# Down products of a sparse expert layer turned round: 256 tokens wide, rounded 32-bit parts, gates applied ahead of the product

## The chip, the cores and the metric

The kernel runs on one core of one Trainium2 chip. A core has a matrix engine (TensorE, PE in the profile, with its weight loads as PEld), a vector engine (VectorE, DVE), an activation engine (ScalarE, ACT), a general engine (GpSimd, POOL) and a queue engine that issues DMAs (SyncE, SP). SBUF is the on-chip memory of 128 partitions, PSUM the eight accumulation banks that TensorE writes. The metric is the device time of one execution in microseconds; the kernel before takes 240.61 us, the median of 3 runs (240.35 to 241.06).

## The reference

One decoder layer on 8 sequences of 128 tokens of width 128, everything in 32-bit floats: causal self-attention with 16 heads, layer norm after the residual, cross-attention with 16 heads of 8, layer norm, then a layer of 8 experts of which a router picks two for each token, and a last layer norm. The part that matters here:

```
x2      = layernorm(x1 + cross_attention(x1, ctx))           # [1024 tokens, 128]
dense_w = sparsemixer(x2 @ router_w.T)                       # [1024, 8], two entries of a row are not 0
for e in range(8):
    h_e  = silu(x2 @ w_gate[e].T) * (x2 @ w_up[e].T)         # [1024, 256]
    out += dense_w[:, e:e+1] * (h_e @ w_down[e].T)           # [1024, 128]
result  = layernorm(x2 + out)
```

The kernel computes every expert for every token.

## The kernel before, in words

Each engine has one long list of calls, written out by hand and tied together by semaphores; nothing reorders them when the kernel runs. The calls are small helpers, and `n` or `l` in them is the sequence.

**Attention part.** Queries, keys and values are projected in three passes of rounded 32-bit numbers: a number is split into a rounded high part and the remainder, and high x high, high x low and low x high are added up in PSUM. Plain 32-bit products do scores, mixing and transposes. The eight sequences are interleaved, self-attention of one beside cross-attention of another. In `normalise_x1` (line 835) VectorE turns `res1` in SBUF into `x1` in SBUF.

**Expert part.** Tokens are taken in four chunks of 256 (`c`, of `NCH`). For each chunk there are 16 blocks of 128 hidden units, two to an expert (`FB`), so `gate_up(i)` runs 64 times (i from 0 to 63). It makes six products of 256 columns, three for the gate and three for the up half, into one bank. The first 32 (`NFILL`) stand in the list among the last calls of the attention part. ScalarE takes the silu of the gate half (`gate`, line 561), VectorE multiplies it with the up half from PSUM (`hidden`, line 935) into `hid`. For the first chunks `hid` lies where the raw weights and the query/key tiles were.

`down_product(c, e)` (line 1988) multiplies the hidden values of one chunk and one expert with the expert's down weights. The hidden values are the stationary side, 128 tokens at a time, and the moving side is 128 output columns wide, in plain 32-bit: four products for an expert, with tokens on the partitions of the result. `combine` (line 1320) on VectorE then multiplies a 128x128 result in PSUM with the gate, a number for each partition, and adds it to a sum in SBUF. In the last chunk the same is done in 16 pieces (`last_product`, line 2001, `combine_last`, line 1332). When a chunk's sum is complete, VectorE makes its statistics, GpSimd raises the variance to the power -1/2 (line 479), VectorE normalises and SyncE sends it out.

The router's choice is worked out once for all tokens by `rank_0` to `rank_9` on VectorE: some 30 steps on 128x64 values in SBUF, laid between the calls `hidden(17)` and `hidden(26)`. GpSimd has nothing to do in this part but `split_x2`, which splits the transposed x2 (lines 353 and 355), and the roots.

In the main loop TensorE makes one down product and two gate/up products in turn; VectorE combines in the same rhythm.

Of the kernel before, what the change touches and what calls it, by code (L numbers as in the profile page):

```python
# [5 lines left out]
F32 = mybir.dt.float32  # L6
F32R = mybir.dt.float32r
# [31 lines left out]
def build_decoder(nc, x, xT, ctxT, mask, wqT, wkT, wvT, woT, cwqT, cwkT, cwvT, cwoT, cbq, cbk, cbv, cbo,  # L39
# [12 lines left out]
    LAST, LAST_E = NCH - 1, 3  # L52
# [18 lines left out]
    NFILL = 32  # L71
    NTANH = 10

    with ExitStack() as ctx:
# [6 lines left out]
        def flat(t):  # L81
# [81 lines left out]
        dense_w = sb("dense_w", [P, B, E])  # L163
        NS = 4
        silu = sb("silu", [P, NS, CH])
        hid = [raw[:].rearrange("p (k t) -> p k t", k=KB),
               qk_a[:].rearrange("p b a k t -> p (b a k) t")]
        free_s = flat(probsT_s)
        acc = free_s[:, 0:2 * TB * D].rearrange("p (c a d) -> p c a d", c=2, a=TB)
        y_out = free_s[:, 2 * TB * D:3 * TB * D].rearrange("p (a d) -> p a d", a=TB)  # L170
# [7 lines left out]
        Y_BANK = [X0, T1, OC]  # L178
        MAIN_BANK = [Y1, X1, OS, T0]

        LAST_UNITS = [(tb, e) for e in range(LAST_E) for tb in range(TB)] + [(tb, e) for tb in range(TB) for e in range(LAST_E, E)]
        LAST_BANK = [Y_BANK[(LAST * E + u) % 3] for u in range(3)] + MAIN_BANK

        FILL_BANK = [Y0, Y1, OS, X1, OC, Y1, T0, X1, T1, Y0, OC, X1, T0, OC, X1, Y0,
                     T0, OS, Y0, X1, OS, X0, OC, T0, Y1, Y0, X1, T1, OS, T0, OC, Y0]
# [8 lines left out]
        def hid_of(b):  # L196
# [18 lines left out]
        (wo_s, res1_done, stat1_done, aggr1_done, var1_done, pow1_done, x1_ready, x1bo_done,  # L215
         x1T_ps, x1T_evac, cq_proj, cq_evac, cq_lower) = [sem(n) for n in (
             "wo_s res1_done stat1_done aggr1_done var1_done pow1_done x1_ready x1bo_done "
             "x1T_ps x1T_evac cq_proj cq_evac cq_lower").split()]
        (oc_evac, oct_ps, rec_c, ccat_done, ccatT_ps, ccatT_evac, wo_c, res2_done, stat2_done, aggr2_done, var2_done, pow2_done,
         x2_ready, x2T_ps, x2T_evac, logit_ps, logit_evac, x2_split) = [sem(n) for n in (  # L220
             "oc_evac oct_ps rec_c ccat_done ccatT_ps ccatT_evac wo_c res2_done stat2_done aggr2_done var2_done pow2_done "
             "x2_ready x2T_ps x2T_evac logit_ps logit_evac x2_split").split()]
        (r_step, r_exp_in, r_exp, dense_ready, gated, silued, gate_done, hid_done, down_ps, combined,
         stat3_done, aggr3_done, var3_done, pow3_done, y_ready) = [sem(n) for n in (
             "r_step r_exp_in r_exp dense_ready gated silued gate_done hid_done down_ps combined "
             "stat3_done aggr3_done var3_done pow3_done y_ready").split()]

        def qk_of(a, pair, which, i):

# [253 lines left out]
        def _(act):  # L483
# [276 lines left out]
            for i in range(2 * KB, NCH * KB):  # L760
                gate(i)
# [1304 lines left out]
```

## Time and profile before

| what | value |
|---|---|
| median of 3 runs | 240.61 us (240.35 to 241.06) |
| profiled execution | 241.12 us, span of the instructions 239.3 us |
| granted TensorE clock, mean | 0.997 |
| TensorE busy | 229.1 us (96%) |
| VectorE busy | 194.4 us (81%) |
| ScalarE busy | 165.7 us (69%) |
| GpSimd busy | 100.9 us (42%) |

TensorE's busy time counts the modelled length of each product, which overlaps the next one; how fast products really follow each other is read from the difference of their start times.
### The profile page before, as it was taken

What the parts mean: (1) busy time and instruction counts of PE and PEld (TensorE: products, weight loads), DVE (VectorE), ACT (ScalarE), POOL (GpSimd) and SP (SyncE); (2) the same over time, 40 slices, a digit from 0 to 9 for tenths busy, and PEclk for the clock granted to TensorE, in tenths of its full rate; (3) what the DMA queues carried; (4) which work ended last, traced back from release to release, by engine and by line L of the source; (5) the groups of instructions that cost most, each with busy time, mean ns of one, the idle gap of its engine ahead of it and who ended that gap; (6) DMA issues with size and microseconds to landing.
All of it is one profiled execution on the core that took longest, in us unless ns stands there. A gap on an engine that the chain in (4) does not pass through costs nothing.

```text
span 239.3 us, 6960 instructions
## 1 busy us (share of the span) xinstructions
PE 229.1 (96%) x2274; PEld 205.8 (86%) x2274; DVE 194.4 (81%) x955; ACT 165.7 (69%) x546; POOL 100.9 (42%) x159
## 2 busy tenths in 40 slices
PE   6899999999999999999999899999999999999992
PEld 6889888887888979978869668797999999999992
DVE  1897799988788889998898985998989755766885
ACT  2769678898989898989989989489448333333000
POOL 3386966465533569808384863302400000100111
PEclk9999999999999999999999999999999999999998
DMA  5997000000000000000000004000000000000000
GB/s 181 358 360 285 9 0 1 4 0 4 3 1 3 0 5 0 3 4 0 4 0 4 0 3 178 0 3 3 1 3 0 0 4 0 4 22 0 22 25 23
DMA packets 6723, 9.10 MB, mean 38 GB/s; under 512 B 1056, under 2 KB 5280, under 8 KB 6304
## 3 DMA queue, kind: packets, MB, share of 16 engines
q1 hardware_dynamic: 4176, 7.09, 8.3%
q10 hardware_dynamic: 2512, 1.57, 2.2%
q8 instruction: 18, 0.29, 0.5%
q14 instruction: 17, 0.14, 0.2%
HBM read 8.14 MB, written 0.52 MB: 36 GB/s over the span
## 4 chain that ended last, share of the span: by engine, by line
PE 83%; DVE 6%; issue 4%; POOL 2%; DMA 2%; ACT 1%; POOLq 0%; SPq 0%; DVEq 0%; ACTq 0%
PE bank L1501 11%; PE bank L1410 10%; PE bank L1411 9%; PE bank L1412 9%; PE bank L1988 7%; PE bank L1483 7%; PE bank L1510 6%; PE bank L1551 6%; PE bank L1494 3%; PE bank L1519 3%; DMA raw<-in_wqT 2%; PE bank L1526 2%; PE bank L1438 2%; PE bank L1440 1%; PE bank L1439 1%
## 5 line engine op out<-in xcount | busy, mean ns | idle before, releaser
L500 ACT ACTIVATE probs_s<-masked_s,nmax_s 128x128 f32<-128x128 f32 x128 | 50.1, 395 | 2.1 <-PE bank L1501 1.1
L296 POOL TENSOR_TENSOR probs_s<-probs_s,rec_sum_s 128x512 f32<-128x512 f32 x32 | 33.2, 1040 | 38.8 <-DVE rec_sum_s L812 38.8
L503 ACT ACTIVATE probs_c<-masked_c,nmax_c 128x128 f32<-128x128 f32 x128 | 40.8, 397 | 1.2 <-DVE nmax_c L805 1.0
L561 ACT ACTIVATE silu<-bank 128x256 f32<-128x256 f32 x54 | 20.3, 387 | 30.0 <-PE bank L1412 28.3
L1410 PE MATMUL bank<-ctx_hi,gu_hi 128*128 128x256 f32 x128 | 38.5, 300 | 0.0
L1411 PE MATMUL bank<-ctx_lo,gu_hi 128*128 128x256 f32 x128 | 35.8, 279 | 0.0
L1412 PE MATMUL bank<-ctx_hi,gu_lo 128*128 128x256 f32 x128 | 35.7, 279 | 0.0
L805 DVE CUSTOM_DVE_ANT_0 masked_c<-bank,mask_add 128x128 f32<-128x128 f32 x128 | 29.3, 286 | 3.7 <-PE bank L1494 2.2
L805 DVE CUSTOM_DVE_ANT_0 masked_s<-bank,causal 128x128 f32<-128x128 f32 x128 | 29.2, 286 | 2.2 <-PE bank L1483 1.8
L479 POOL TENSOR_TENSOR mv<-mv,minus_half 128x1 f32<-128x1 f32 x8 | 4.3, 548 | 58.6 <-DVE mv L1352 58.6
L1410 PEld LDWEIGHTS bank<-ctx_hi,gu_hi 128*128 128x128 f32 x128 | 24.2, 189 | 0.5 <-issue 0.4
L500 ACT ACTIVATION_READ_ACCUMULATOR probs_s<-masked_s,nmax_s 128x1 f32 x128 | 24.5, 191 | 0.0
L1411 PEld LDWEIGHTS bank<-ctx_lo,gu_hi 128*128 128x128 f32 x128 | 24.2, 189 | 0.0
L1412 PEld LDWEIGHTS bank<-ctx_hi,gu_lo 128*128 128x128 f32 x128 | 24.1, 188 | 0.0
L542 ACT COPY xT_all<-bank 128x512 f32<-128x512 f32 x32 | 18.3, 581 | 6.0 <-PE bank L1501 5.5
L1410 PE MATMUL bank<-x_hi,w_hi 128*128 128x256 f32 x64 | 19.9, 312 | 0.7 <-DVE w_lo L772 0.7
L1501 PE MATMUL bank<-ident,probs_c 128*128 128x128 f32 x128 | 19.5, 278 | 0.0
L1501 PE MATMUL bank<-ident,probs_s 128*128 128x128 f32 x128 | 19.0, 276 | 0.2 <-POOL probs_s L296 0.2
L1411 PE MATMUL bank<-x_lo,w_hi 128*128 128x256 f32 x64 | 18.0, 282 | 0.0
L1412 PE MATMUL bank<-x_hi,w_lo 128*128 128x256 f32 x64 | 18.0, 282 | 0.0
L935 DVE TENSOR_TENSOR qk_a<-silu,bank 128x256 f32<-128x256 f32 x32 | 12.8, 419 | 6.4 <-ACT silu L561 6.1
L1510 PE MATMUL bank<-probsT_s,v_sb 128*64 128x128 f32 x256 | 17.5, 279 | 0.0
(165 smaller groups left out, 589.3 us busy)
## 6 DMA issues: line engine op xcount, KB each, us to landing
raw<-in_gateT SPq DMA_DIRECT2D x1, 1024.0 KB, 8.6
raw<-in_upT SPq DMA_DIRECT2D x1, 1024.0 KB, 11.7
down_sb<-in_down SPq DMA_DIRECT2D x1, 1024.0 KB, 4.8
raw<-in_wvT SPq DMA_DIRECT2D x1, 512.0 KB, 6.3
ctxT_all<-in_ctxT SPq DMA_DIRECT2D x1, 512.0 KB, 7.6
wo_sb<-in_woT SPq DMA_DIRECT2D x1, 512.0 KB, 6.2
masked_c<-in_mask ACTq DMA_DIRECT2D x1, 512.0 KB, 11.2
x_tok<-in_x ACTq DMA_DIRECT2D x1, 512.0 KB, 9.8
```

The lines of the kernel that those rows point to most:

```text
L296: pool.tensor_tensor(probs_s[:, g % 2], probs_s[:, g % 2], spread(rec_sum_s[:, 4 * g:4 * g + 4], 2, S), ALU.mult).then_inc(normed[g], 1)
L500: last = act.activation(probs_s[:, g % 2, i, :], masked_s[:, g % 2, i, :], ACT.Exp, scale=-1.0, bias=nmax_s[:, h:h + 1], accum_out=rsum_s[ ...
L503: last = act.activation(probs_c[:, g % 2, i, :], masked_c[:, g % 2, i, :], ACT.Exp, scale=-1.0, bias=nmax_c[:, h:h + 1])
L542: act.copy(dst[:, g % 2].rearrange("p h t -> p (h t)"), b[:]).then_inc(turned_evac[kind][g], 1)
L561: act.activation(silu[:, i % NS, :], g, ACT.Silu).then_inc(silued, 1)
L805: last = dve.tensor_tensor_reduce(out=masked[:, g % 2, i, :], in0=b[:, i * S:(i + 1) * S], in1=add, scale=-1.0, scalar=3e38, op0=ALU.add, ...
L1410: pe.matmul(dst, wh, xh, start=True, stop=False)
L1411: pe.matmul(dst, wh, xl, start=False, stop=False)
L1412: return pe.matmul(dst, wl, xh, start=False, stop=True)
L1483: ins = pe.matmul((even, odd)[r][:, i * S:(i + 1) * S], qk_of(a, pair, 0, i)[rows, toks], qk_of(a, pair, 1, i)[rows, toks], start=True, st ...
L1501: last = pe.transpose(b[:, i * S:(i + 1) * S], (probs_s if kind == "s" else probs_c)[:, g % 2, i, :], ident[:])
L1510: last = pe.matmul(b[DQ * r:DQ * (r + 1), i * S:(i + 1) * S], v_sb[:, 8 * a + 2 * i + r, :], probsT_s[:, r, i, :], start=True, stop=True)
```

## The change

**What it does.** The down weights become the stationary side and 256 tokens the moving side. Each product is now made in three passes of rounded 32-bit parts, six of 256 columns for an expert, and all eight experts of a chunk are added up in one PSUM bank, with output columns on the partitions. For that the hidden values must carry their gate before the product. New steps, in the order of the data:

- `turn_gates` (TensorE) and `evac_gates` (VectorE) turn `dense_w` to 64 rows of 128 tokens. SyncE writes them to memory and loads each half chunk's rows back spread over all partitions, eight loads of 512 KB into tiles that are no longer in use (`gate_w`).
- `scale(k)` (VectorE, 32 times, k is chunk x 8 + expert) multiplies the hidden values of an expert, 128x512, by the gates, in place.
- `high_part(k)` (ScalarE, 32 times) rounds them into a ring of seven (`NRING`).
- `lower(k)` makes the remainder: GpSimd for 23 of them, VectorE for the odd k from 15 on (`LOW_DVE`).
- `split_down` (GpSimd, 8 instructions) splits the down weights.
- `down_product(k)` (TensorE) waits for the low part.
- When a chunk's bank is complete, ScalarE copies it out in two halves (`evac_yT`), TensorE adds x2 into two fresh banks by a product with the identity (`residual_of_y`) and turns the copied halves on top (`turn_yT`). Statistics and normalisation read PSUM. `combine` and `combine_last` are gone.

The hidden values of different experts now lie in places of their own, so `hidden` no longer waits for the down products of two chunks earlier. TensorE's list after gate/up 31 is: 20 gate/up products (`NAHEAD`) with the gates' turning after the first, six times a down product and two gate/up products (`NPAIRED`), then 26 down products.

The calls up to gate/up 31 are the same on every engine, in a new order and with other banks. The diff, cut to its core:

```diff
+    NAHEAD = 20
+    NPAIRED = (NCH * KB - NFILL - NAHEAD) // 2
+    LOW_DVE = tuple(range(15, NCE, 2))
...
+            sp.wait_ge(late_evac, 1)
+            sp.dma_start(gate_dram, gate_rows).then_inc(gates_out, 16)
+            sp.wait_ge(gates_out, 32)
+            for c in range(NCH):
+                for h in range(2):
+                    rows = gate_dram[(2 * c + h) * E:(2 * c + h + 1) * E, :].rearrange("(a r) t -> a (r t)", a=1)
+                    sp.dma_start(gate_w[2 * c + h].rearrange("p e t -> p (e t)"), rows.broadcast_to([P, E * S])).then_inc(ld_gates[c][h], 16)
...
+            def split_down(n):
+                rows = slice(4 * n, 4 * n + 4)
...
+                pool.tensor_copy(down_hi[:, rows, :], down_sb[:, rows, :]).then_inc(parts_done, 1)
+                pool.wait_ge(parts_done, 2 * n + 1)
+                pool.tensor_tensor(down_lo4[n], down_sb[:, rows, :], down_hi[:, rows, :].bitcast(F32),
+                                   ALU.subtract).then_inc(parts_done, 1)
+
+            def lower(k):
+                pool.wait_ge(high_done, k + 1)
+                pool.tensor_tensor(low[k % NRING], hid[k], high[k % NRING].bitcast(F32), ALU.subtract).then_inc(parts_done, 1)
...
+            for n in range(KB // 4):
+                split_down(n)
+            for k in range(NCE):
+                if k not in LOW_DVE:
+                    lower(k)
+                for c in range(NCH - 1):
+                    if k == (22, 30, 31)[c]:
+                        root_of_y(c, 0)
+                        root_of_y(c, 1)
...
+            def high_part(k):
+                act.wait_ge(scaled, k + 1)
+                wait(act, down_ps, k - NRING + 1)
+                act.activation(high[k % NRING], hid[k], ACT.Copy).then_inc(high_done, 1)
...
+            def scale(k):
+                c, e = k // E, k % E
+                dve.wait_ge(ld_gates[c][e // 4], 32 if c == 0 else 48)
+                dve.wait_ge(hid_done, (k + 1) * FB)
+                dve.tensor_tensor(hid[k], hid[k], spread(gate_w[2 * c + e // 4][:, e % 4, :], 1, FB), ALU.mult).then_inc(scaled, 1)
+
+            def lower(k):
+                dve.wait_ge(high_done, k + 1)
+                dve.tensor_tensor(low[k % NRING], hid[k], high[k % NRING].bitcast(F32), ALU.subtract).then_inc(low_dve, 1)
...
+            for j in range(NPAIRED):
+                i = NFILL + NAHEAD + 2 * j
+                hidden(i)
+                scale(2 * j + 6)
+                hidden(i + 1)
+                scale(2 * j + 7)
...
+            normalise_y(1)
+            statistics_of_y(2)
+            normalise_y(2)
+            statistics_of_y(LAST)
+            normalise_y(LAST)
...
+            def down_product(k):
...
+                wait_low(pe, k)
+                for f in range(FB):
+                    j = e * FB + f
+                    pe.matmul(out, down_hi[:, j, :], high[k % NRING][:, f, :], start=(e == f == 0), stop=False)
+                    pe.matmul(out, down_hi[:, j, :], low[k % NRING][:, f, :], start=False, stop=False)
+                    last = pe.matmul(out, down_lo[j], high[k % NRING][:, f, :], start=False, stop=(e == E - 1 and f == FB - 1))
...
+            gate_up(NFILL)
+            turn_gates()
+            for i in range(NFILL + 1, NFILL + NAHEAD):
+                gate_up(i)
+            for j in range(NPAIRED):
+                down_product(j)
+                gate_up(NFILL + NAHEAD + 2 * j)
+                gate_up(NFILL + NAHEAD + 2 * j + 1)
+            for k in range(NPAIRED, NCE):
+                down_product(k)
+                if k in (11, 19, 29):
+                    residual_of_y(k // E - 1)
+                    turn_yT(k // E - 1)
+            residual_of_y(LAST)
+            turn_yT(LAST)
```

**How the lists read.** VectorE in the main loop before, where `silu,bank` are the two inputs of `hidden` (`bank` is PSUM, all other names are SBUF) and the second line is `combine`:

```order
L935 TENSOR_TENSOR raw<-silu,bank 128x256 x2
L1320 SCALAR_TENSOR_TENSOR probsT_s<-bank,dense_w,probsT_s 128x128 x2
L935 TENSOR_TENSOR raw<-silu,bank 128x256 x2
L1320 SCALAR_TENSOR_TENSOR probsT_s<-bank,dense_w,probsT_s 128x128 x2
L935 TENSOR_TENSOR raw<-silu,bank 128x256 x2
```

VectorE in the changed kernel, from the last paired period on; L1041 is `hidden`, L1423 `scale`, L1427 `lower`:

```order
L1041 TENSOR_TENSOR raw<-silu,bank 128x256
L1423 TENSOR_TENSOR x_tok<-x_tok,cvp 128x512
L1041 TENSOR_TENSOR raw<-silu,bank 128x256
L1423 TENSOR_TENSOR x_tok<-x_tok,cvp 128x512
L1423 TENSOR_TENSOR v_sb<-v_sb,cvp 128x512 x2
L1427 TENSOR_TENSOR w_lo<-qk_a,w_hi 128x512
L1423 TENSOR_TENSOR catT<-catT,masked_c 128x512
L1427 TENSOR_TENSOR w_lo<-x_tok,w_hi 128x512
```

An instruction that reads PSUM has given way to ones that read two tiles of SBUF.

GpSimd at the end of its list before, from the last splits of x2 (L353, L355) on:

```order
L353 CAST ctx_hi<-x2T_cur 128x128
L355 TENSOR_TENSOR ctx_lo<-x2T_cur,ctx_hi 128x128
L479 TENSOR_TENSOR mv<-mv,minus_half 128x1 x8
L74 UNCONDITIONAL_BRANCH
```

And in the changed kernel, from the same place (L406 and L408 are the last split of x2, L533 and L535 `split_down`, L540 `lower`):

```order
L406 CAST ctx_hi<-x2T_cur 128x128
L408 TENSOR_TENSOR ctx_lo<-x2T_cur,ctx_hi 128x128
L533 CAST k_own<-down_sb 128x512
L535 TENSOR_TENSOR down_more<-down_sb,k_own 128x512
...
L533 CAST k_own<-down_sb 128x512
L535 TENSOR_TENSOR x_hi<-down_sb,k_own 128x512
L540 TENSOR_TENSOR w_lo<-raw,w_hi 128x512 x6
L540 TENSOR_TENSOR x_lo<-raw,x_hi 128x512
L540 TENSOR_TENSOR w_lo<-raw,w_hi 128x512
L540 TENSOR_TENSOR w_lo<-qk_a,w_hi 128x512 x5
```

Where eight roots stood there are now 8 splitting and 23 subtracting instructions with the roots between the last of them.

## Rows read from the trace of the kernel before

**Rows 1.** Windows: stretch, length, then busy us (count) PE, PEld, DVE, ACT, POOL; clock, DMA
```profile
100.00:140.00 40.00, 38.38 (x420) 31.68 (x422) 36.42 (x212) 37.24 (x137) 23.12 (x32) 1.00 0.01 2
...
200.00:210.00 10.00, 10.00 (x89) 10.00 (x89) 7.00 (x27) 3.09 (x8) 1.06 (x2) 1.00 0.01 2
```

**Rows 2.** Waits, 180 to 240 us: who waited for whom, total us, times, longest
```profile
ACT silu L561 <- PE bank L1412: 22.8, 30, 1.2
```

**Rows 3.** Timeline of PE, 201 to 205 us: start, length, instruction, count
```profile
201.33 1.05 PE L1988 MATMUL bank<-down_sb,qk_a 128*128 128x128 f32 x8
...
202.46 0.28 PE L1412 MATMUL bank<-ctx_hi,gu_lo 128*128 128x256 f32 x1
...
203.51 0.27 PE L1412 MATMUL bank<-ctx_hi,gu_lo 128*128 128x256 f32 x1
203.63 1.05 PE L1988 MATMUL bank<-down_sb,qk_a 128*128 128x128 f32 x8
```

**Rows 4.** Timeline of PE: the first down product and the last chunk's
```profile
182.96 1.05 PE L1988 MATMUL bank<-down_sb,raw 128*128 128x128 f32 x8
...
227.81 7.00 PE L2001 MATMUL bank<-down_sb,qk_a 128*128 128x128 f32 x60
```

**Rows 5.** Groups by line and form, 180 to 240 us: count, busy us, mean ns, idle before
```profile
L1320 DVE SCALAR_TENSOR_TENSOR probsT_s<-bank,dense_w,probsT_s 128x128 f32<-128x128 f32 x42 | 12.5, 345 | 0.8 <-PE bank L1988 0.8
...
L561 ACT ACTIVATE silu<-bank 128x256 f32<-128x256 f32 x38 | 14.2, 386 | 23.4 <-PE bank L1412 22.8 <-DVE qk_a L935 0.6
```

**Rows 6.** Groups by form, whole span: the nearest forms to those added
```profile
L490 ACT ACTIVATE w_hi<-raw 128x512 fp32r<-128x512 f32 x2 | 1.2, 625 | 0.6 <-DMA raw<-in_wqT 0.6
...
L346 POOL TENSOR_TENSOR gu_lo<-raw,gu_hi 128x512 fp32r<-128x512 f32 x8 | 10.3, 1283 | 0.6
...
L344 POOL CAST gu_hi<-raw 128x512 fp32r<-128x512 f32 x8 | 4.9, 610 | 0.0
...
L779 DVE TENSOR_TENSOR ctx_lo<-ctxT_all,ctx_hi 128x512 fp32r<-128x512 f32 x2 | 1.3, 673 | 0.0
```

**Rows 7.** Timelines of DVE and POOL around 16, 119, 134 and 150 us
```profile
15.62 0.20 POOL L336 TENSOR_TENSOR cb_sum<-cb_own 128x4 f32<-128x4 f32 x1
15.82 0.66 DVE L779 TENSOR_TENSOR ctx_lo<-ctxT_all,ctx_hi 128x512 fp32r<-128x512 f32 x1
15.89 0.64 POOL L337 TENSOR_TENSOR cb_nat<-cb_sum 128x2 f32<-128x2 f32 x1
16.40 0.68 DVE L876 COPY qk_a<-bank 128x512 f32<-128x512 f32 x1
...
118.93 1.03 POOL L296 TENSOR_TENSOR probs_s<-probs_s,rec_sum_s 128x512 f32<-128x512 f32 x1
119.00 1.05 DVE L835 TENSOR_SCALAR x<-res,mv 128x128 f32<-128x128 f32 x1 [0.24 <-POOL mv L360]
...
133.92 0.46 POOL L355 TENSOR_TENSOR ctx_lo<-x2T_cur,ctx_hi 128x128 fp32r<-128x128 f32 x1
134.25 1.21 DVE L835 TENSOR_SCALAR x<-res,mv 128x128 f32<-128x128 f32 x1
134.33 1.04 POOL L296 TENSOR_TENSOR probs_s<-probs_s,rec_sum_s 128x512 f32<-128x512 f32 x1
...
150.56 0.35 DVE L835 TENSOR_SCALAR x<-res,mv 128x128 f32<-128x128 f32 x1
```

**Rows 8.** Timeline of PE at 136 us: the transpose of x1
```profile
136.12 0.33 PE L1556 MATMUL bank<-ident,x 128*128 128x128 f32 x1 [1.02 <-DVE v_sb L881]
```

**Rows 9.** Timelines of POOL and DVE at 174 us: last split, a routing step
```profile
173.65 0.46 POOL L355 TENSOR_TENSOR ctx_lo<-x2T_cur,ctx_hi 128x128 fp32r<-128x128 f32 x1
...
174.21 0.23 DVE L969 TENSOR_TENSOR r_a<-logits,r_m 128x64 f32<-128x64 f32 x1
```

**Rows 10.** Timeline of DVE at the end: statistics and normalisation of the last half
```profile
235.55 0.29 DVE L1342 BATCH_NORM_STATS2 stat<-probsT_s 128x6 f32<-128x128 f32 x1
...
237.04 0.34 DVE L1359 TENSOR_SCALAR probsT_s<-probsT_s,mv 128x128 f32<-128x128 f32 x1 [0.66 <-POOL mv L479]
```

**Rows 11.** DMA issues: tile, queue, count, KB each, us to landing
```profile
down_sb<-in_down SPq DMA_DIRECT2D x1, 1024.0 KB, 4.8
```

More of the change, by code:

```diff
@@ new lines, in build_decoder @@
+        half = FB * CH
+        high, low = [[t[:, i:i + half].rearrange("p (k t) -> p k t", k=FB) for t, n in ((w[:].rearrange("p a c -> p (a c)"), 6), (x[:], 1))
+                      for i in range(0, n * half, half)] for w, x in ((w_hi, x_hi), (w_lo, x_lo))]
+        NRING = len(high)
+        down_more = sb("down_more", [P, 12, D], F32R)
+        down_hi = k_own[:].rearrange("p a b s t -> p (a b s t)").rearrange("p (k d) -> p k d", k=KB)
+        down_lo = [down_more[:, k, :] for k in range(12)] + [x_hi[:, half + k * D:half + (k + 1) * D] for k in range(4)]
@@ new lines, in build_decoder, with wait_low @@
+        parts_done, scaled, high_done, low_dve, yT_evac, late_ps, late_evac = [
+            sem(n) for n in "parts_done scaled high_done low_dve yT_evac late_ps late_evac".split()]
+        gates_out, ld_gates = ld_wqk[4], ((ld_wqk[0], ld_wqk[5]),) + tuple((s, s) for s in ld_wqk[1:NCH])
+        def wait_low(eng, k):
+            if k in LOW_DVE:
+                eng.wait_ge(low_dve, LOW_DVE.index(k) + 1)
+            else:
+                eng.wait_ge(parts_done, KB // 2 + k + 1 - len([j for j in LOW_DVE if j < k]))
@@ L921, in hidden @@
                 dve.wait_ge(silued, i + 1)
-                wait(dve, down_ps, (c - 2) * E + k // FB + 1 if c >= 2 else 0)
+                if i == LAST * KB:
+                    dve.wait_ge(parts_done, KB // 2)
+                if c == LAST and k >= KB // 2 and k % FB == 0:
+                    wait_low(dve, (k - KB // 2) // FB)
                 if c == 0:
@@ new lines, in _ @@
+            for j in range(NPAIRED):
+                i = NFILL + NAHEAD + 2 * j
+                hidden(i)
+                scale(2 * j + 6)
+                hidden(i + 1)
+                scale(2 * j + 7)
+            for j in range(NCE - 2 * NPAIRED - 6):
+                scale(2 * NPAIRED + 6 + j)
+                if j % 3:
+                    lower(LOW_DVE[j - 1 - j // 3])
+                if j == 6:
+                    statistics_of_y(0)
+                elif j == 8:
+                    normalise_y(0)
+                elif j == 12:
+                    statistics_of_y(1)
@@ new lines, in residual_of_y, with turn_yT @@
+            def residual_of_y(c):
+                for tb in range(TB):
+                    b = c * TB + tb
+                    if c == 0:
+                        pe.wait_ge(hid_done, NCH * KB)
+                        pe.wait_ge(late_evac, 1)
+                    wait(pe, y_ready, b - 2 * TB + 1)
+                    pe.matmul(Y_TOK_BANK[c % 2][tb][:, 0:D], ident[:], x2_all[:, b, :], start=True, stop=False)
+            def turn_yT(c):
+                for tb in range(TB):
+                    pe.wait_ge(yT_evac, c * TB + tb + 1)
+                    pe.matmul(Y_TOK_BANK[c % 2][tb][:, 0:D], yT[:, c % 2, tb * P:(tb + 1) * P], ident[:], start=False,
+                              stop=True).then_inc(late_ps, 1)
```

1691 lines of the change are left out of this document (825 added, 866 removed).

## Prediction

> **What bounds the kernel now.** I read the table of windows first, then the waits after 180 us, then TensorE's timeline. TensorE is busy for 38.4 of 40 us in the attention part and for all of 200 to 210 us, at the full granted clock, while VectorE has 7.0 and ScalarE 3.1 of 10 us in that last stretch [rows 1]. ScalarE idled 22.8 us in all after 180 us, and always for TensorE's last gate/up product [rows 2]. So in the expert part the other engines have room, and a shorter TensorE list would shorten the kernel as long as the others keep up. What must be checked is whether they do.
>
> One period of the main loop is one down product and two gate/up products: 201.33 to 203.63, 2.30 us [rows 3]. Nine rounded 32-bit products of 256 columns go from 202.46 to 203.51, so one takes 0.117 us; twelve are 1.40 us, and the down product (eight passes in the trace) takes the other 0.90 us.
>
> **TensorE's own sum.** A down product becomes six rounded products, 0.70 us. Before, 24 of them cost 24 x 0.90 = 21.6 us and the last eight 7.2 us (a stretch of 7.0 us at 64 passes [rows 4], rounded up for its missing records). Now 32 cost 22.4 us: 6.4 us less. Added are eight residual and eight turning products of the plain 32-bit kind at 0.225 us (a quarter of 0.90), and the turning of the gates at 0.3: 3.9 us. If nothing else mattered TensorE would be done 2.5 us sooner.
>
> **A gap at the first down product.** It follows directly on gate/up 51, but its low half hangs on gate 50 on ScalarE (0.39), the rounding there (0.63, by the nearest row, the rounding of a weight piece of the same shape) and the subtraction on GpSimd (1.28) [rows 5, 6]. With some 0.3 us of handing over these start when gate/up 50 ends, 0.70 us before 51 does. TensorE stands still for about 1.9 us.
>
> **The other engines, each alone.** VectorE loses 64 combinations of 0.35 us [rows 5] and gets 32 scalings and nine subtractions of 128x512 at 0.67 us, where the next instruction can start 0.55 to 0.6 us later [rows 6, 7]. ScalarE gets 32 roundings. GpSimd gets 23 subtractions of 1.28 us and, after its last x2 split, four roundings of 0.61 and four subtractions of the down weights [rows 6]. Per period of the six paired ones (TensorE 2.1 us) that is 1.9 us on VectorE, 1.6 to 2.0 on ScalarE and 2.5 on GpSimd; GpSimd may be late there, for it has stock to build until the 26 unpaired products, of which it then serves every second one. Each alone would just do.
>
> **Where it breaks: VectorE and GpSimd together.** In the front, VectorE's x1 normalisation (SBUF in, SBUF out) takes 0.35 us when GpSimd is quiet. Started at 119.00, 0.07 us behind a GpSimd multiplication of 1.03 us, it took 1.05, and ended 0.09 us after that one. Started at 134.25 it took 1.21 us and outlasted two GpSimd instructions; the TensorE transpose that wanted it came 1.02 us late [rows 7, 8]. The lock goes the other way too, and with an instruction of the very form that is added: from 15.82 VectorE runs a tensor-tensor with both inputs in SBUF, and GpSimd's addition of two columns, begun at 15.89, takes 0.64 us where the one before it, of four columns, took 0.20 [rows 7]. So a VectorE instruction with two SBUF inputs and a GpSimd one exclude each other. Before, that cost little because the gated product and the combination each read one input from PSUM. Now the scaling and the subtraction on VectorE read both from SBUF, and run exactly while GpSimd subtracts.
>
> The Trainium skill ("SBUF — State Buffer", section "SBUF: two separate sides") says the same: the pair of ports that VectorE and GpSimd share is an exclusive lock, taken also by a VectorE instruction with two SBUF inputs, and the loser waits for the whole instruction. By that rule, the trace agrees (the 1.05 and 0.64 us above). Engines that only shared bandwidth would give the first rival below.
>
> Priced: 41 VectorE instructions x 0.55 = 22.6 us and 23 on GpSimd x 1.24 (1.28 less what overlaps) = 28.5 us, 51 us of exclusive use, which begins with the scaling after gate/up 46. TensorE alone has about 40 us of work from there.
>
> Walking through it:
> - The fill ends at 182.96 [rows 4]. GpSimd is free from 174.1, and the routing steps on VectorE (0.23 us each, most with two SBUF inputs) begin at 174.21 [rows 9]. Now GpSimd's eight instructions for the down weights (7.6 us) lie upon them. Each can hold up one routing step by about 0.7 us, 5 us in all, and a gate/up product waits for VectorE to empty its bank. VectorE is some 2 us behind there already but not late. I take 3 us of delay, bounds 0 and 5.
> - Gate/up 32 to 51 and the gates: 14.3 us. Then the gap, 2.3 us with the lock. The first down product starts at 182.96 + 3 + 14.3 + 2.3 = 202.6.
> - Six paired periods: two scalings and two subtractions exclude each other, 2 x (0.55 + 1.24) = 3.6 us instead of 2.1: 21.5 us.
> - Left are 14 scalings, nine VectorE and about ten GpSimd subtractions, 12.6 + 12.4 us of exclusive use. About 3 us more go where one side waits for a rounding, for statistics, or for two roots: 28 us until the last low half.
> - After it VectorE still has, in its order, normalise 1, statistics 2, normalise 2, statistics 3, normalise 3. Before, one half took 1.5 us from statistics to normalisation, and 2.3 us from the start of its last one to the end [rows 10]. Two halves take about 2.3: 0.5 + 2.3 + 2.3 + 1.9 = 7.0 us.
>
> End: 202.6 + 21.5 + 28 + 7.0 = 259.1 us of span, against 239.3. The profiled execution of before took 241.12 us with that span; its runs have a median of 240.61. Adding the difference of 19.8 to the median gives 260.4, and I say 260.0.
>
> **The gates' way through memory.** One write of 32 KB and eight loads of 512 KB, all behind each other on SyncE's queue, where the outputs stand behind them. 1024 KB took 4.8 us from issue to landing [rows 11]. Written, read and landed, the first is there some 6 us after gate/up 32, while the first scaling comes 10 us after it: nothing. If reading one row for 128 partitions were three times slower, the second chunk's gates would be some 5 us late; the lock has used up that time by then.
>
> **The new call order.** Each engine makes the same calls up to gate/up 31. The stall of 1.02 us [rows 8] and its like add up to 2 or 3 us on TensorE between 100 and 170 us. A new order may lose or double them: between -3 and +3, I take 0.
>
> **Rivals.**
> 1. The two engines hardly hinder each other. Then the down phase goes at TensorE's pace: 197.3 + 1.9 = 199.2 for its start, 12.6 for six periods, and 20.6 until the last low half (14 scalings, nine subtractions and one set of statistics fill VectorE there), then 7.0: 239.4, a time of 240.7. With up to 3 us from the order it ends between 237.5 and 243. Its gain on TensorE is eaten by the gap and by the serial end. For it speaks that a small GpSimd share (0 to 1 of 10 us) is all the trace shows late; against it the 1.05 and 1.21 us.
> 2. Only part is exclusive, for example because GpSimd takes inputs in pieces and lets VectorE in between. Half of the extra goes: 239.4 + 10 = 249.4, a time of 250.7. Against it speaks that the wait lasted until GpSimd's end each time.
> 3. Faster: the lock is harmless and the order removes the stalls of the front, which are the lock's own [rows 7, 8]. Then about 3 us off rival 1: a span of 236.5, a time of 237.8. That decides if VectorE's scaling stays at 0.67 us beside a busy GpSimd.
>
> **How the numbers follow.** The lock as priced has 0.84, with its own range 251 to 267: from no delay in the fill and no idle time in the last part, to 5 us in the fill and GpSimd winning twice running. Rival 2 has 0.07, rival 1 (without 3) 0.06, rival 3 0.03. The range 249 to 267 holds most of the first two and leaves 0.15 outside. This kernel's measurement tells 0.3% (0.7 us) from no change. Faster has rival 3 and part of rival 1: 0.05. Same has 0.04. Slower has the rest, 0.91.
>
> **What would show it.** In the profile after: VectorE's scalings with a mean well above 0.67 us (1.3 or more while GpSimd works); GpSimd's subtractions lengthened where they come second; paired periods of 3.4 to 3.8 us; TensorE's busy share in the last quarter falling from 10 of 10 to about 6; routing steps of up to 1.3 us beside the splitting of the down weights. Six rounded products in 0.70 us when they run together. It is wrong if scalings stay at 0.67 us, or if TensorE waits for the gates' loads.

## The result, and the profile after

| | before | after |
|---|---|---|
| median | 240.64 us (240.35 to 241.06, 4 runs) | 258.51 us (257.54 to 259.21, 4 runs) |
| ratio | | 1.0738, 95% interval 1.0693 to 1.0784 |
| span of the profiled execution | 239.3 us | 257.4 us |
| TensorE, VectorE, GpSimd busy | 229.1, 194.4, 100.9 us | 233.4, 222.3, 148.2 us |

The time forecast was 260.0 us. In the runs gate_psum and gate_psum_split_late below, one and two executions were in a slower state of the core; the medians given for them include these (without them 244.01 and 239.69 us), the ratios do not. I read the windows first, as before the change. The columns are the stretch, its length, busy us (count) of PE, PEld, DVE, ACT and POOL, the granted clock, and DMA. First one long window of the attention part, then the changed kernel from the routing on:

```profile
20.00:140.00 120.00, 120.00 (x1325) 104.60 (x1325) 106.06 (x617) 111.53 (x411) 79.44 (x105) 1.00 0.05 18
...
160.00:170.00 10.00, 8.61 (x73) 8.34 (x72) 9.06 (x29) 4.78 (x11) 5.16 (x9) 1.00 0.01 2
170.00:180.00 10.00, 7.55 (x51) 7.35 (x50) 9.38 (x26) 4.86 (x9) 4.21 (x5) 0.83 0.01 2
180.00:190.00 10.00, 9.82 (x85) 9.65 (x85) 7.36 (x23) 5.97 (x17) 0.00 (x0) 1.00 0.26 68
190.00:200.00 10.00, 7.96 (x66) 7.78 (x66) 8.24 (x17) 5.20 (x14) 2.34 (x2) 0.97 0.93 356
200.00:210.00 10.00, 10.00 (x76) 10.00 (x76) 8.74 (x12) 6.27 (x15) 7.63 (x6) 0.86 0.00 2
210.00:220.00 10.00, 8.41 (x63) 7.42 (x61) 10.00 (x13) 5.97 (x14) 10.00 (x7) 1.00 0.01 2
220.00:230.00 10.00, 6.55 (x45) 5.63 (x46) 10.00 (x9) 3.16 (x5) 8.71 (x7) 1.00 0.00 0
```

TensorE has no gap in this window of the attention part, where it had some in [rows 1]. It loses 3.8 us beside the routing (160 to 180) and again from 210 us on, where VectorE is busy without a break and GpSimd nearly so. In [rows 1] VectorE had 7.0 of 10 us there.

The timeline of VectorE, then that of GpSimd, in the paired stretch of the changed kernel (start, length, instruction):

```profile
203.07 0.68 DVE L1423 TENSOR_TENSOR raw<-raw,qk_b 128x512 f32<-128x512 f32 x1
203.73 0.42 DVE L1041 TENSOR_TENSOR down_sb<-silu,bank 128x256 f32<-128x256 f32 x1
204.07 1.39 DVE L1423 TENSOR_TENSOR raw<-raw,qk_b 128x512 f32<-128x512 f32 x1
205.38 0.41 DVE L1041 TENSOR_TENSOR down_sb<-silu,bank 128x256 f32<-128x256 f32 x1
205.71 1.45 DVE L1423 TENSOR_TENSOR qk_a<-qk_a,wo_sb 128x512 f32<-128x512 f32 x1
207.09 0.41 DVE L1041 TENSOR_TENSOR down_sb<-silu,bank 128x256 f32<-128x256 f32 x1
207.42 1.46 DVE L1423 TENSOR_TENSOR qk_a<-qk_a,wo_sb 128x512 f32<-128x512 f32 x1
```
```profile
203.30 6.74 POOL L540 TENSOR_TENSOR w_lo<-raw,w_hi 128x512 fp32r<-128x512 f32 x4 [2.37 <-ACT w_hi L839]
209.99 1.75 POOL L540 TENSOR_TENSOR x_lo<-raw,x_hi 128x512 fp32r<-128x512 f32 x1
```

A scaling (L1423) takes 0.68 us when GpSimd is quiet, or when GpSimd starts later than it, as at 203.07. Beside GpSimd's low halves (L540), four of which take 6.74 us instead of 4 x 1.28 [rows 6], it takes 1.39 to 1.46 us, while the hidden part (L1041), which reads one input from PSUM, keeps its 0.41. From 205.71 to 207.42 one product's share is 1.71 us on VectorE, so a paired period, which has two of them, is 3.42 us there.

### The profile page after: what moved, and what is told of

Its sections match the earlier page's. It is cut to its first block, busy times and chain, and to the rows that moved or that the text cites. A ratio compares the mean times of both kernels' runs of the same rounds, so it can differ in the third digit from the quotient of the medians.

```text
span 257.4 us, 6928 instructions
## 1 busy us (share of the span) xinstructions
PE 233.4 (91%) x2243; PEld 210.0 (82%) x2243; DVE 222.3 (86%) x933; ACT 183.5 (71%) x586; POOL 148.2 (58%) x190
## 4 chain that ended last, share of the span: by engine, by line
PE 70%; DVE 18%; issue 6%; POOL 3%; ACT 1%; DMA 1%; DVEq 0%; POOLq 0%
PE bank L1571 12%; PE bank L1480 7%; PE bank L1553 7%; PE bank L1482 7%; PE bank L1481 7%; PE bank L1580 6%; PE bank L1621 6%; PE bank L1589 4%; PE bank L1564 3%; DVE qk_a L1423 2%; DVE qk_a L1041 2%; PE bank L1637 2%; PE bank L1508 2%; DVE w_lo L1427 2%; PE bank L1509 1%
## 5 line engine op out<-in xcount | busy, mean ns | idle before, releaser
L1481 PE MATMUL bank<-ctx_lo,gu_hi 128*128 128x256 f32 x128 | 36.8, 288 | 0.0
L1482 PE MATMUL bank<-ctx_hi,gu_lo 128*128 128x256 f32 x128 | 36.8, 287 | 0.0
L540 POOL TENSOR_TENSOR w_lo<-raw,w_hi 128x512 fp32r<-128x512 f32 x9 | 15.3, 1721 | 29.4 <-ACT w_hi L839 29.4
L1480 PEld LDWEIGHTS bank<-ctx_hi,gu_hi 128*128 128x128 f32 x128 | 25.6, 200 | 6.0 <-DVE qk_a L1041 4.2
L2071 PE MATMUL bank<-w_hi,k_own 128*128 128x256 f32 x56 | 17.8, 317 | 10.3 <-POOL w_lo L540 6.3
L1481 PEld LDWEIGHTS bank<-ctx_lo,gu_hi 128*128 128x128 f32 x128 | 25.3, 198 | 0.0
L1482 PEld LDWEIGHTS bank<-ctx_hi,gu_lo 128*128 128x128 f32 x128 | 25.2, 197 | 0.0
L2071 PEld LDWEIGHTS bank<-w_hi,k_own 128*128 128x128 f32 x56 | 11.2, 200 | 12.4 <-POOL w_lo L540 6.6
L1480 PE MATMUL bank<-x_hi,w_hi 128*128 128x256 f32 x64 | 19.3, 301 | 0.0
L1571 PE MATMUL bank<-ident,probs_c 128*128 128x128 f32 x128 | 18.7, 275 | 0.0
L1571 PE MATMUL bank<-ident,probs_s 128*128 128x128 f32 x128 | 18.7, 276 | 0.0
```

The costliest lines, as they stand in the source:

```text
L1480: pe.matmul(dst, wh, xh, start=True, stop=False)
L1481: pe.matmul(dst, wh, xl, start=False, stop=False)
L1482: return pe.matmul(dst, wl, xh, start=False, stop=True)
L1571: last = pe.transpose(b[:, i * S:(i + 1) * S], (probs_s if kind == "s" else probs_c)[:, g % 2, i, :], ident[:])
L2071: pe.matmul(out, down_hi[:, j, :], high[k % NRING][:, f, :], start=(e == f == 0), stop=False)
```

## The experiments

All medians are of three rounds, each beside the kernel before (240.8 to 241.0 us). The names are those of the runs.

### The lock alone: gate_psum

```
- dve.tensor_tensor(hid[k], hid[k], spread(gate_w[...][:, e % 4, :], 1, FB), ALU.mult)
+ dve.tensor_tensor(hid[k], hid[k], T1[:].rearrange("p (k t) -> p k t", k=FB), ALU.mult)
```

> The changed kernel, but each of the 32 scalings on VectorE reads its second input from an idle PSUM bank instead of the gates' tile in SBUF, so the values are not weighted by the gates; same count, shape and order, and only the nine low parts on VectorE still read two tiles of SBUF. Theory (VectorE instructions with two SBUF inputs and GpSimd exclude each other): scalings fall from 1.44 us to about 0.69, GpSimd's low parts from 1.74 to 1.28, paired periods from 3.42 to 2.1 to 2.6 us; first down product still at about 199 us; time 241 to 246. Rival (the time is lost in the chain scale, round, subtract, multiply and the ring of seven, whatever the inputs are): no change, 256 to 259.

Measured: 244.32 us, ratio 1.0133 (1.0107 to 1.0159), 14.2 us less than the changed kernel with the same number of instructions. The same stretch of VectorE:

```profile
204.41 0.68 DVE L1423 TENSOR_TENSOR qk_a<-qk_a,bank 128x512 f32<-128x512 f32 x1
205.25 0.42 DVE L1041 TENSOR_TENSOR raw<-silu,bank 128x256 f32<-128x256 f32 x1 [0.16 <-ACT silu L637]
205.59 0.68 DVE L1423 TENSOR_TENSOR qk_a<-qk_a,bank 128x512 f32<-128x512 f32 x1
```

Scalings of 0.68 us throughout. GpSimd's low halves take 1.28 us in the paired stretch. They go up to 1.84 us only later, where they meet VectorE's own low halves, which still read twice from SBUF. So neither the work on SBUF nor the number of instructions made the scalings long, but where the second input lies.

### The split beside the routing: split_late

```
  if n == 0:
      pool.wait_ge(ld_down, 16)
      pool.wait_ge(scored["c"][NG - 1], B)
+     pool.wait_ge(dense_ready, 1)
```

> The changed kernel, but GpSimd starts splitting the down weights only when the gates are worked out (one wait more). Theory: the routing steps on VectorE fall back to 0.22 us each (now up to 1.34), TensorE loses its 3 to 4 us of idle time between 168 and 176 us, and the splitting (7.6 us) still ends before the first low part is wanted: 254 to 256. Rival (those stalls come from the new order of calls): no change, 258 to 259, or slower if the splitting is then late.

Measured: 252.78 us, ratio 1.0493 (1.0461 to 1.0525): 5.7 us less than the changed kernel. The routing steps in the changed kernel, and then in this one:

```profile
167.39 1.32 DVE L1066 TENSOR_TENSOR probs_c<-logits,r_m 128x64 f32<-128x64 f32 x1
...
169.59 1.04 DVE L1070 TENSOR_TENSOR probs_c<-pos_e,r_m 128x64 f32<-128x64 f32 x1
```
```profile
166.99 0.23 DVE L1067 TENSOR_TENSOR probs_c<-logits,r_m 128x64 f32<-128x64 f32 x1
...
168.10 0.23 DVE L1071 TENSOR_TENSOR probs_c<-pos_e,r_m 128x64 f32<-128x64 f32 x1
```

In the changed kernel GpSimd's split ran from 167.36 for 1.27 us and from 169.26 for 1.29, and each of the two steps ended 0.08 us after it. The gain is larger than forecast (254 to 256 us). The forecast counted only TensorE's idle time, but its clock comes back too: between 170 and 180 us the granted clock was 0.83 in the changed kernel and is 1.00 here, and TensorE makes 76 products instead of 51.

### Both lifted: gate_psum_split_late

The two edits above together.

> The changed kernel with both of its losses lifted: the scaling takes its second input from a PSUM bank that lies idle (values other than the gates, so the output differs), and the split of the down weights on GpSimd starts only when the last gates are there. My theory: gate_psum alone took 14.2 us off 258.5, split_late alone 5.7, and they stand in different stretches (the expert part and the routing), so they add up but for 1 us or so: 238.5 us (237.5 to 240), scalings of 0.68 us, a paired period near 2.11 us, routing steps of 0.22 us. Rival 1: the later split now stands in the way, since the first down product can start sooner than its weights are split: the first down product after 194.6 us, in all 241 or more. Rival 2: with the lock away nothing is left of the new down products' cost: as order_only, 235 us.

Measured: 239.79 us, ratio 0.9974 (0.9937 to 1.0011). The two losses add up but for 1.2 us: 258.5 - 239.8 = 18.7 us against 14.2 + 5.7. The first down product came at 193.45 where split_late had it at 194.63, so the later split is not in the way.

### The order alone, and the down part alone: order_only, down_only

order_only has the new order of calls and banks up to gate/up 31 and the old expert part behind it; down_only the reverse.

```
order_only   - Y_BANK = [X0, T1, OC]      + Y_BANK = [X0, OC, T0]
             - round_ctx(1)               + split_x(2)
             - split_cwk()                + split_x(3)
             ...
down_only    the lists of calls before gate/up 32 as they were
```

> The new order of calls up to gate/up 31 alone, with the expert part of before (plain 32-bit down products, combination on VectorE, no splitting on GpSimd). Gate/up 16 started at 165.3 us in the changed kernel and at 171.0 before. Theory (the order brings time, the lock in the fill took it away again): 234.5 to 238. Rival (the order brings nothing): 240 to 241.5.

> The new down products, scalings and splittings with the old order of calls. Theory: the loss of the changed kernel and, on top, what its order brought: 261 to 266. Rival (the loss lies in the new order): 250 or less.

Measured: order_only 235.05 us, ratio 0.975 (0.9727 to 0.9773), which beats both kernels; down_only 266.18 us, 1.1041 (1.0988 to 1.1094). The page of order_only, waits of TensorE over the first 180 us (who waited for whom, total, times, longest):

```profile
PE bank L1567 <- POOL causal L375: 2.2, 1, 2.2
```

That is the start of the kernel. The transpose that came 1.02 us late in [rows 8] has no successor, and the longest x1 normalisation takes 585 ns instead of 1214. The order is worth more than I took it for in the prediction (0, between -3 and +3): 6.0 us with the old expert part and 7.7 with the new (266.2 against 258.5), so that down_only ended just above its forecast.

### Less help, more speed: all_low_dve

split_late with GpSimd's 23 low halves moved to VectorE:

```
- LOW_DVE = tuple(range(15, NCE, 2))
+ LOW_DVE = tuple(range(NCE))
...
  hidden(i)
+ lower(2 * j + 1)
  scale(2 * j + 6)
...
```

The other low halves and the statistics are placed anew in the same list.

> split_late with all 32 low halves on VectorE (GpSimd keeps the roots only), in the order hidden, low half, hidden, low half of the paired stretch; nothing else is moved off or added. VectorE gets 23 instructions more of the kind that takes about 0.68 us undisturbed, GpSimd loses as many of 1.72 us. My theory (the two exclude each other): a scaling and a low half together are 1.36 us undisturbed against the 1.705 us that a pair takes now, so the kernel with less help is faster: 32 x 0.34 = 11 us less, less than 3 us given back since low halves now stand ahead of hidden parts in the paired stretch: 244 us (242 to 248), against 252.8 for split_late; scalings 0.68 us and low halves 0.68 us throughout. Rival: GpSimd's half of the low parts is real help and the long scalings have another cause (a busy SBUF, ScalarE's copies): scalings stay over 1.2 us, VectorE has 23 x 1.3 us more to do, 265 us or more.

Measured: 249.94 us, ratio 1.0366 (1.0346 to 1.0386): 2.8 us less than split_late, by doing 23 x 0.69 us more on the busiest engine. VectorE's timeline:

```profile
203.13 0.68 DVE L1428 TENSOR_TENSOR w_lo<-raw,w_hi 128x512 fp32r<-128x512 f32 x1
203.73 0.69 DVE L1424 TENSOR_TENSOR qk_a<-qk_a,wo_sb 128x512 f32<-128x512 f32 x1
204.34 0.41 DVE L1042 TENSOR_TENSOR down_sb<-silu,bank 128x256 f32<-128x256 f32 x1
204.67 0.69 DVE L1428 TENSOR_TENSOR w_lo<-raw,w_hi 128x512 fp32r<-128x512 f32 x1
```

One product's share is 1.54 us against 1.71. The gain was forecast at 8.8 us and was 2.8. The forecast compared 1.36 us with 1.705 and left out that the hidden part is within the 1.705: the true difference was 0.17 and not 0.34. And the first low half now stood behind six scalings, so the first down product came at 196.23 instead of 194.63.

### What GpSimd must read: pool_copy

split_late with a plain copy in place of GpSimd's subtraction; the low parts hold other values.

```
- pool.tensor_tensor(low[k % NRING], hid[k], high[k % NRING].bitcast(F32), ALU.subtract)
+ pool.tensor_copy(low[k % NRING], hid[k])
```

> split_late with GpSimd's 23 low halves replaced by plain copies of the same size into the same place (one SBUF input; the low parts hold other values, so the output differs). Theory A, the lock is held by any GpSimd instruction for as long as it lasts: a copy is 0.61 us alone against 1.28 us for the subtraction, scalings that meet one take 1.2 to 1.3 us, and the pair of scaling and copy goes from 1.705 us to about 1.3 us: 22 x 0.4 = 9 us off 252.8, 244 us (242 to 246). Theory B, only GpSimd instructions with two SBUF inputs exclude VectorE's: scalings of 0.68 us, 239 us as gate_psum_split_late. Theory C, GpSimd's instruction count and not its length matters: no gain, 251 us or more.

Measured: 239.72 us, ratio 0.9939 (0.9924 to 0.9954), the time of theory B. Groups of the two lines (count, busy us, mean ns, idle before), of VectorE and then of GpSimd:

```profile
L1424 DVE TENSOR_TENSOR raw<-raw,qk_b 128x512 f32<-128x512 f32 x8 | 5.7, 715 | 0.0
```
```profile
L541 POOL CAST w_lo<-raw 128x512 fp32r<-128x512 f32 x9 | 8.7, 985 | 14.7 <-ACT w_hi L840 14.5
```

These copies take 0.985 us instead of the 0.61 of [rows 6], so they do meet the scalings, and the timelines tell how. A little later in this run, from 210 us on, no hidden part stands between VectorE's two-input instructions. VectorE, then GpSimd:

```profile
210.26 1.07 DVE L1428 TENSOR_TENSOR w_lo<-qk_a,w_hi 128x512 fp32r<-128x512 f32 x1 [0.51 <-ACT w_hi L840]
211.25 1.09 DVE L1424 TENSOR_TENSOR catT<-catT,masked_c 128x512 f32<-128x512 f32 x1
212.26 1.09 DVE L1428 TENSOR_TENSOR w_lo<-x_tok,w_hi 128x512 fp32r<-128x512 f32 x1
```
```profile
210.17 0.62 POOL L541 CAST w_lo<-qk_a 128x512 fp32r<-128x512 f32 x1
210.80 1.00 POOL L541 CAST w_lo<-x_tok 128x512 fp32r<-128x512 f32 x1
```

VectorE's instruction of 210.26 started 0.09 us behind a copy that ended at 210.79, and ended itself at 211.33, 0.54 us later: it did nearly all of its 0.68 us behind the copy. The next copy waited for it, and the next scaling for that copy. So a copy holds VectorE up just as a subtraction does, for as long as it lasts, which is theory A. In the paired stretch VectorE always has a hidden part of 0.33 us between two scalings, and most of the copy fits in there: its scalings take 0.68 and 0.77 us in turn. Five copies in a row take 5.16 us from 202.84, 1.03 us each, while TensorE needs 2.11 / 2 = 1.05 us for a product. The lock is still there, but it is no longer what limits. Theory A had the right mechanism and the wrong sum (a pair of 1.3 us, 244 us in all). Theory B has the right time and the wrong mechanism, which is luck.

### Where VectorE reads PSUM: pool_busy and pool_busy_22

order_only with 30 and with 22 subtractions of 128x512 added on GpSimd in the expert part, one for each down product, results unused:

```
+ for n in range(30):           # pool_busy_22: range(22)
+     pool.wait_ge(combined, 2 * n + 1)
+     pool.tensor_tensor(x_lo[...], x_hi[:, 512:1024], x_hi[:, 0:512], ALU.subtract)
```

> order_only with 30 subtractions of 128x512 with two SBUF inputs added on GpSimd in the expert part, one for every down product, results unused. There VectorE has only instructions with one SBUF input (hidden part and combination read PSUM for the other). My theory: the lock needs a two-SBUF-input instruction on VectorE too, so nothing waits: GpSimd instructions of 1.28 us, VectorE's as in order_only, 235 to 236 us. Rival 1: any VectorE instruction is held up by GpSimd's two-input instructions: combinations and hidden parts (0.35 to 0.4 us) go over 1 us where they meet one, 30 x 0.9 = 27 us of VectorE, 245 us or more. Rival 2: the GpSimd subtractions load SBUF as a whole and slow all engines by a few per cent: 238 us.

> pool_busy with 22 of the 30 subtractions, the last eight gone, so that GpSimd has none left when the powers for the last two chunks are due; nothing else changes. In pool_busy VectorE's hidden parts and combinations kept their 0.42 and 0.34 us, yet it took 7 us more than order_only; my theory is that these 7 us are the powers queued behind subtractions on GpSimd (VectorE's normalisation waited 5.6 us for them) and one normalisation of 1.28 us instead of 0.34, not a load on SBUF: 235.5 us (235 to 237). Rival: GpSimd's subtractions slow the kernel while they run, wherever the powers stand: 240 us (22 thirtieths of 7 us over 235).

Measured: 242.09 us (ratio 1.0039, 1.0023 to 1.0054) and 238.44 us (0.9894, 0.9852 to 0.9936), both above the forecasts of my theory (235 to 236 and 235 to 237). The groups of the first show that the instructions I had named are not held up:

```profile
L1328 DVE SCALAR_TENSOR_TENSOR probsT_s<-bank,dense_w,probsT_s 128x128 f32<-128x128 f32 x40 | 11.9, 343 | 0.8 <-PE bank L2001 0.8
L943 DVE TENSOR_TENSOR qk_a<-silu,bank 128x256 f32<-128x256 f32 x16 | 6.6, 420 | 5.8 <-ACT silu L569 5.8
L1367 DVE TENSOR_SCALAR probsT_s<-probsT_s,mv 128x128 f32<-128x128 f32 x8 | 5.1, 650 | 5.6 <-POOL mv L478 5.6
```

343 and 420 ns, as in order_only. What I had left out is the last row: the normalisation of the output reads and writes SBUF, and it waited for powers queued behind subtractions. In the second run one such place is left. VectorE, then GpSimd:

```profile
218.13 0.34 DVE L1368 TENSOR_SCALAR probsT_s<-probsT_s,mv 128x128 f32<-128x128 f32 x1 [1.02 <-POOL mv L478]
218.65 1.27 DVE L1368 TENSOR_SCALAR probsT_s<-probsT_s,mv 128x128 f32<-128x128 f32 x1 [0.17 <-POOL mv L478]
```
```profile
217.55 1.07 POOL L478 TENSOR_TENSOR mv<-mv,minus_half 128x1 f32<-128x1 f32 x2
218.58 1.27 POOL L487 TENSOR_TENSOR x_lo<-x_hi 128x512 fp32r<-128x512 f32 x1
```

The normalisation started 0.07 us behind the subtraction and ended with it, 0.93 us late, and the power before it was 1.02 us late. TensorE then waited 2.2 us for VectorE. Up to 214 us this kernel keeps the period of [rows 3] (2.29 us here, 2.30 there) with a subtraction in each. So both forecasts missed because they left the normalisation out, in whole or for one place, and the lock is seen once more, with a one-input instruction from SBUF to SBUF. The waits named make 2.2 of the 3.4 us. The windows behind them show most of the rest (the granted clock is the last number but two):

```profile
222.00:224.00 2.00, 2.00 (x12) 2.00 (x11) 0.97 (x4) 0.00 (x0) 2.00 (x3) 0.50 0.03 8
224.00:226.00 2.00, 2.00 (x14) 2.00 (x14) 1.21 (x6) 0.00 (x0) 1.21 (x1) 0.64 0.00 0
226.00:230.00 4.00, 4.00 (x39) 4.00 (x38) 3.50 (x16) 0.00 (x0) 1.07 (x2) 1.00 0.09 27
```

After the wait TensorE makes 26 products in 4.0 us, where it then makes 39: some 1.3 us more, my estimate. In order_only its clock is 1.00 from 220 to 226.

### A whole kernel with the gates in PSUM: gates_in_psum

ScalarE copies the gates of two experts into the idle bank, and VectorE scales two parts behind each other.

```
+ act.copy(T1, gate_w[2 * c + e // 4][:, e % 4:e % 4 + 2, :])
...
  scale(2 * j + 6)
- hidden(i + 1)
  scale(2 * j + 7)
+ hidden(i + 1)
...
```

The later split of split_late is in it too.

> The whole computation, with the scaling's second input in PSUM: ScalarE copies the spread gates of two experts (128x512, some 0.63 us by its rounding of that size) into the idle bank before VectorE scales the two parts, which therefore stand together in VectorE's order; the split of the down weights starts after the last gates. My theory (the length of the scalings is GpSimd's two-input subtraction against VectorE's two-input instruction from SBUF): scalings 0.68 us, GpSimd's low halves about 1.35 us; against gate_psum_split_late (239.8) it adds 16 copies on ScalarE, of which some 1 to 3 us reach TensorE since the copy and the scaling may not touch the bank together: 241.5 us (239.5 to 245), about the kernel before. Rival: ScalarE cannot take 10 us more in the paired stretch, or the alternation of copy and scaling holds VectorE up: 248 us or more, with scalings still 0.68.

Measured: 254.0 us, ratio 1.0545 (1.0501 to 1.0588). A clear miss, on the rival's side: scalings are 0.68 us, and yet the kernel is no faster than split_late with 252.78. ScalarE's and then VectorE's timeline:

```profile
206.75 0.59 ACT L843 COPY bank<-cv_all 128x512 f32<-128x512 f32 x1 [0.96 <-DVE qk_a L1442]
207.27 0.63 ACT L848 ACTIVATE w_hi<-raw 128x512 fp32r<-128x512 f32 x1
207.81 0.36 ACT L638 ACTIVATE silu<-bank 128x256 f32<-128x256 f32 x1
```
```profile
206.56 0.41 DVE L1060 TENSOR_TENSOR raw<-silu,bank 128x256 f32<-128x256 f32 x1
208.21 0.42 DVE L1060 TENSOR_TENSOR raw<-silu,bank 128x256 f32<-128x256 f32 x1 [1.24 <-ACT silu L638]
```

With one bank, copy and scaling take turns; ScalarE stands 0.96 us for the scalings, its activation comes late behind the copy, and VectorE stands 1.24 us for that. The copies repeat every 3.2 us instead of the 2.1 us that TensorE needs. One wait was traded for another. A version with two banks was not tried.

### What is left of the fill: down_only_split_late, down_only_turn_late

The fill was forecast for the old order, so its term is measured there. First the wait of split_late in down_only; then, on top of it:

```
- gate_up(NFILL); turn_gates()
+ if i == NFILL + 3: turn_gates()
```

> down_only (the old order of calls with the new down part, 266.2 us) with the split of the down weights on GpSimd put off until the last gates are there, as in split_late. It measures the term of the fill of my prediction by itself, which was worked out for the old order: 3 us, bounds 0 and 5. In down_only the first down product came at 207.1 where that working has 199.6 without a delay, 7.5 us. Theory 1: all of that is the split lying on the routing steps, four of which take 1.0 to 1.3 us instead of 0.23 and let TensorE stand still and its clock fall: 259.5 us (258.5 to 260.5), first down product near 200. Theory 2: the split costs 5.7 us there too, as under the new order, and the rest is something else of the new down part: 260.5 us or a little more, first down product at 201.5 or later. Theory 3: the split costs what I forecast, 3 us: 263 us.

> down_only_split_late (261.2 us) with TensorE turning the gates, and VectorE emptying them, after gate/up 35 and no longer after gate/up 32. It tests what is left of the fill: in down_only_split_late TensorE stood for 2.01 us before that turning, since the gates are the router's last step and VectorE still had the router and its hidden parts to do, and its granted clock fell to 0.85 in 180 to 190 us. The kernel before had no such wait, since its gates were wanted only at the first combination. My theory: the wait goes, the gates' loads start some 2 us later and still land ahead of the first scaling: first down product at 200.5 to 201.2 instead of 203.19, 258.8 us (258 to 260). Rival: the four banks of the gate/up products are full by then and TensorE waits as long at gate/up 36, or the scalings wait for the loads: 261 us.

Measured: 261.22 us (ratio 1.0829, 1.0801 to 1.0856) and 258.76 us (1.0749, 1.0727 to 1.077). The first is nearest to theory 2: the split costs 5.0 us here, and something is left. The second is as forecast. Timeline of TensorE: the turning of the gates in the first, then the first down product in the second.

```profile
186.02 0.27 PE L2054 MATMUL bank<-ident,dense_w 128*64 128x128 f32 x1 [2.01 <-DVE qk_a L1042]
```
```profile
200.44 0.36 PE L2067 MATMUL bank<-w_hi,k_own 128*128 128x256 f32 x1 [2.05 <-POOL w_lo L541]
```

The first down product comes at 207.12 in down_only, 203.19 with the later split and 200.44 with the later turning too. The working of the prediction has 199.6 without any delay.

## Why the prediction was right, and where its steps were not

**The lock: right.** It had been priced at 19.7 us (259.1 against the first rival's 239.4); lifting both of its places gave back 18.7. A product's share of exclusive use was taken as 0.55 + 1.24 = 1.79 us and was 1.71: the paired period was forecast at 3.6 us and was 3.42 on VectorE. From the first down product at 199.38 to the end of the last low half at 249.01 it was 49.6 us, against 21.5 + 28 = 49.5. The parts lie less well than the sum. VectorE began the 14 scalings that are left at 222.38, after 23.0 us, since its first paired hidden part waited 1.26 us, until 202.74, for ScalarE's activation; the last part then took 26.6 us. And TensorE did not go at the paired pace of VectorE. It found low halves in stock, made three of its six paired periods in 2.1 us each and was through all six at 215.19. Only behind them did it wait for low halves, 11 times and 8.8 us in all.

**One row was read too simply.** The TensorE transpose of [rows 8] waited, as its row says, for VectorE's copy of v (L881), which stood behind the long normalisation in VectorE's list, and not for the normalisation itself. The delay still comes from the lock, at second hand.

**The serial end: mis-sized.** 249.01 to 257.4 is 8.4 us, not 7.0. The end of the changed kernel on VectorE:

```profile
249.45 0.93 DVE L1445 TENSOR_SCALAR probsT_s<-bank,mv 128x128 f32<-128x128 f32 x2 [0.44 <-POOL mv L544]
...
252.03 0.73 DVE L1445 TENSOR_SCALAR probsT_s<-bank,mv 128x128 f32<-128x128 f32 x2 [0.84 <-DMA out<-probsT_s]
...
254.58 0.73 DVE L1445 TENSOR_SCALAR probsT_s<-bank,mv 128x128 f32<-128x128 f32 x2 [1.01 <-POOL mv L544]
```

The working gave the first normalisation 0.5 us; it took 0.44 of waiting and 0.93. It also had no wait for the output of the chunk two before to leave its buffer, 0.84 us.

**The fill and the order: two errors that cancelled, which was luck.** The first down product was forecast at 202.6 and came at 199.38. I had taken 3 us for the fill (bounds 0 and 5) and 0 for the order (-3 to 3). In the old order the fill cost 7.5 us. The split made 3.9 of them, within my bounds. What I had not seen is the turning of the gates, 2.8 us: I counted its 0.3 us of work, and not that it stands behind gate/up 32 in TensorE's list, while its input is the router's last step and its bank is emptied by a hidden part that VectorE has behind the router. In the row of 186.02 above that hidden part (L1042) is what came last; the gates had been ready since 184.2. The kernel before wanted the gates only at its first combination, so no row of it shows a wait there, but the list of the changed kernel does. And the order gave back 6.0 to 7.7 us. Its stalls had been added up as 2 or 3 us of waits; TensorE's busy time by windows of 20 us in the first 180 grew by 3.2 us. The rest of the gain does not show as idle time, and I leave its cause open.

**Rival 1** had the right sign of its parts and the wrong price for the new down part. Without the lock the changed kernel takes 239.8 us, as forecast (237.5 to 243), but only thanks to the order: against order_only with 235.05 the new down products still cost 4.7 us. TensorE's busy time fell from 226.2 to 225.0 us; the gap at the first down product is 1.74 us, and the end behind the last low half is 7.9 us with hardly any TensorE work.

**The gates' loads: right.** The first 512 KB took 4.6 us to land, the later ones, queued behind them, up to 10.9, and nothing waited for them. In down_only_turn_late they are issued later still, at no cost.

## What to carry to other kernels

Before work is given to VectorE and GpSimd at the same time, look where each instruction's inputs lie. One operand in PSUM made the same scaling 0.68 instead of 1.45 us, and leaving GpSimd idle was faster than its help. A short instruction on GpSimd does no harm if it fits beside one of VectorE's that reads PSUM. When a step is moved earlier in one engine's list, price what it waits for, not only what it does. And test an order of calls apart from the arithmetic that came with it: here a gain of 6 us was buried under a loss of 24.

## What the runs showed of the hardware

- VectorE and GpSimd, both with two inputs in SBUF, back to back: the record of the scaling grows from 0.68 to 1.45 us and that of the subtraction from 1.28 to about 1.7, although each pair needs only 1.71 us: both records hold the wait for the other. By start times alone, 0.60 + 1.24 = 1.84 us of work fit into 1.71, so some 0.13 us of a pair overlapped.
- The Trainium skill ("SBUF — State Buffer", section "Who interferes with whom") has the one that comes second blocked until the first has finished. The single meetings agree (1.27 us of VectorE ending with the 1.27 of GpSimd). By that rule a pair would take 1.84 us; the runs have 0.13 less.
- A copy on GpSimd excludes them too: begun 0.09 us before VectorE's instruction, it made that one 1.07 instead of 0.68 us. Where a hidden part stands between scalings, it lengthened them by only 0.04 us on the average of the group shown, and was itself lengthened by 0.37.
- After TensorE had stood still for 2.45 us (to 175.47) and for 2.04 us (to 199.38), its granted clock was 0.50, which is 1.2 GHz, for the next few us. The windows of the changed kernel:

```profile
176.00:178.00 2.00, 2.00 (x12) 2.00 (x11) 1.85 (x8) 1.36 (x2) 0.00 (x0) 0.50 0.03 8
...
199.40:202.70 3.30, 3.30 (x15) 3.30 (x16) 2.08 (x3) 0.38 (x2) 1.53 (x1) 0.50 0.03 10
203.00:206.00 3.00, 3.00 (x28) 3.00 (x27) 3.00 (x6) 2.40 (x7) 2.70 (x2) 1.00 0.00 0
```

15 products in 3.3 us against 28 in 3.0 us: such a wait costs TensorE more than its own length, here some 1.6 us more by my estimate.
